# Two images instead of four summed by TensorE, and an earlier row of finishes on VectorE

## Chip, cores and metric

One Trainium2 chip, one of its cores. The metric is the device time of one launch in microseconds (us), as the median of the runs shown.

## What is computed

The input `x` has 16 images of 128 channels and 32 x 32 pixels, in fp32.

```python
cA, cH, cV, cD = dwt2(x)                     # one level of the Haar wavelet
rimg0 = idwt2(proc(cA), proc(cH), proc(cV), proc(cD))   # 1x1 conv, batch norm, ReLU on each band
rimg1 = idwt2(r2, h1, v1, d1)                # three levels there and back: x again
y = conv3x3(concat([rimg0, rimg1])) + convW_b
x = batchnorm_relu(y, bnW_gamma, bnW_beta)   # the second batch norm, over all 16 images
x_denoised = median_blur(x, 3)               # median of each 3x3 neighbourhood, zero padding
out = x + einsum('bchw,oc->bohw', x_denoised, W) + b
```

## The kernel before

Channels lie on the 128 partitions, so an image is a tile of 128 x 1024. The engines run programs written out by hand, which meet at semaphores; nothing schedules them but the order of the code.

The first 364 us are the wavelet, the first batch norm and the 3x3 convolution on TensorE (PE). VectorE (DVE) takes the medians of the *unnormed* convolution output while PE convolves the images behind it, since a batch norm with its sign taken out keeps the order of the values. The 16 images are cut into 20 units (images 0, 1, 14 and 15 in halves); `median` runs once per unit, in 18 DVE instructions (L780 to L842).

This case is about the end, after the last convolution matmul. There the second batch norm's scale and shift become known (`second_batch_norm`, L884 to L908 on DVE), and then for each image `n`, in order:

- ScalarE (ACT) norms the median, `norm_median` (L622).
- GpSimd (POOL) zeroes the four corner pixels (L348), which releases PE; for an image in `OWN` it then makes the normed image itself in place, `map_x1` (L339).
- PE multiplies the median by `w2`, `mix` (L469), into one of the two halves of `conv_ps`, by turns. `mix(n)` therefore waits until the product of image `n-2` has been read.
- DVE adds the image, the product and the bias, `finish` (L914), and SyncE (SP) sends the image out.

For an image in `SUMMED` the way is another: ACT makes the normed image (L627), PE adds it to the product by a multiplication with a unit matrix (L472), and ACT carries the sum out (L630). Neither POOL's `map_x1` nor DVE's `finish` runs for it.

DVE comes to this end with three pieces of median work still to do: the second half of image 14 (rows of 128x288 and 128x576), the first half of image 15 (128x224 and 128x448) and its second half (288 and 576 again). Its instructions are counted as they are issued (all but L781, L823 and the closing L842 of a whole image); `second_batch_norm` is put after the counted step `BN3_AT`, and one `finish` after each counted step in `FINISH_AT`, for the images of `OWN` in turn. Below, "step 16" is a counted step. Steps 1 to 15 lie in the first of the three pieces, 16 to 31 in the second, 32 to 46 in the third. What is left of the finishes follows the last median. The median of image 15 is whole only then, so ACT, POOL, PE, DVE and SP take it through in a row after it.

Thirty matmuls of zeros (L479) keep PE busy between the last convolution matmul and the first `mix`.

Of the kernel before, what the change touches and what calls it, by code (L numbers as in the profile page):

```python
# [5 lines left out]
def wavelet_conv_median_kernel(nc, x, w1_t, w3_t, w2_t, vectors, out):  # L6
# [39 lines left out]
    BY_POOL = tuple(n for n in range(IMAGES) if n not in BY_DVE)  # L46


    SUMMED = (3, 6, 9, 12)
    OWN = [n for n in range(IMAGES) if n not in SUMMED]  # L50

    BN3_AT, FINISH_AT = 7, (16, 19, 22, 25, 28, 31, 34, 37, 40)


    HALVED = (0, 1, IMAGES - 2, IMAGES - 1)
# [11 lines left out]
    with ctx:  # L67
# [122 lines left out]
        def slot(n):  # L190
            first = n * (ROWS * W) + W
            return y[:, first:first + PIX]

        def zslot(n):
            return z[:, n, :]
# [31 lines left out]
        def _(sp):  # L227
# [17 lines left out]
            for n in range(IMAGES - 1):  # L245
                if n in SUMMED:
                    sp.wait_ge(out_by_act, SUMMED.index(n) + 1)
                else:
# [104 lines left out]
        def _(pe):  # L353
# [108 lines left out]
            def mix(n, k):  # L462
                if n > 0:
                    pe.wait_ge(med_ready, n)
                for b in range(2):
# [3 lines left out]
                    mm = nc.tensor.matmul(conv_ps[:, k, half], w2[:, :], zslot(n)[:, half], start=True, stop=n in OWN)  # L469
                    if n in SUMMED:  # L470
                        pe.wait_ge(x1_by_act, SUMMED.index(n) + 1)
                        mm = nc.tensor.matmul(conv_ps[:, k, half], unit[:, :], slot(n)[:, half], start=False, stop=True)  # L472
# [12 lines left out]
            for n in range(2, IMAGES):  # L485
                if n - 2 in SUMMED:
                    pe.wait_ge(out_by_act, SUMMED.index(n - 2) + 1)
# [475 lines left out]
```

## Time and profile before

| | |
|---|---|
| median of 3 runs | 418.46 us (416.7, 418.46, 418.57) |
| the profiled execution's own time | 418.77 us |
| its span in the profile | 416.3 us |
| busy over the span | PE 402.1, DVE 371.4, POOL 192.2, ACT 157.3 us |
| mean granted PE clock | 0.996 of 2.4 GHz |

The span reaches from the first to the last instruction of the core; the own time has 2.5 us more around it. Busy times overlap, so they say who is loaded, not who is waited for.

### The profile page before, as it was taken

The page shows a single profiled execution, that of the slowest core. Times are in us where ns is not written, and L with a number is a line of the kernel's source. Part 1 is how long each engine was busy: PE and PEld are TensorE (multiplying, and loading weights), DVE is VectorE, ACT ScalarE, POOL GpSimd, SP SyncE. Part 2 cuts the span into 40 slices and gives each one's busy share as a digit, 9 for nine tenths or more (in the row PEclk, how much of TensorE's full clock was granted, in tenths as well). Part 3 has the DMA queues.
Part 4 walks back from the last instruction along what each step waited for, and adds up shares of the span by engine and source line. Part 5 has one row for each costly group of instructions (what it writes and reads, how often), then busy time and mean ns, then how long its engine had stood idle before and what let it go on. Part 6 is the DMA issues. An engine that isn't in the chain of part 4 may idle for free.

```text
span 416.3 us, 3679 instructions
## 1 busy us (share of the span) xinstructions
PE 402.1 (97%) x1142; PEld 213.1 (51%) x1142; DVE 371.4 (89%) x528; ACT 157.3 (38%) x352; POOL 192.2 (46%) x196
## 2 busy tenths in 40 slices
PE   7889999999999999999999999999999999997994
PEld 2334578956444444444444444444446688843441
DVE  2899866999849999999999998989898999988995
ACT  1466663422253432323232323141413322373861
POOL 3999386531715543435554443434343440032341
PEclk9999999999999999999999999999999999999998
DMA  7980110010101011010101010100100000003654
GB/s 282 418 333 3 47 54 2 9 41 0 53 0 50 1 50 30 22 50 0 50 2 51 0 50 3 50 14 37 39 13 2 0 0 2 0 0 151 252 211 193
DMA packets 7794, 26.70 MB, mean 64 GB/s; under 512 B 992, under 2 KB 1248, under 8 KB 7776
## 3 DMA queue, kind: packets, MB, share of 16 engines
q1 hardware_dynamic: 7776, 26.48, 16.7%
q8 instruction: 9, 0.15, 0.2%
q14 instruction: 9, 0.07, 0.1%
HBM read 18.09 MB, written 8.39 MB: 64 GB/s over the span
## 4 chain that ended last, share of the span: by engine, by line
PE 86%; DVE 7%; ACT 2%; issue 2%; DMA 1%; POOL 1%; SPq 0%; POOLq 0%; DVEq 0%; ACTq 0%
PE conv_ps L380 75%; PE conv_ps L469 4%; PE one_ps L362 4%; PE one_ps L445 2%; PE conv_ps L472 1%; DVE z L660 1%; DVE z L661 1%; DVE stats L666 1%; DMA z<-x 1%; DVE y L914 1%; POOL y L339 1%; ACT z L622 1%; ACT sorted_cols L503 0%; ACT y L627 0%; ACT y L630 0%
## 5 line engine op out<-in xcount | busy, mean ns | idle before, releaser
L380 PE MATMUL conv_ps<-ru,wt 128*128 128x512 f32 (+1 forms) x360 | 131.2, 500 | 0.0
L380 PEld LDWEIGHTS conv_ps<-ru,wt 128*128 128x128 f32 x360 | 68.2, 190 | 53.3 <-issue 50.2
L380 PE MATMUL conv_ps<-xu,wt 128*128 128x496 f32 (+3 forms) x240 | 87.4, 500 | 0.0
L573 ACT ACTIVATE y<-conv_ps,sgn 128x512 f32<-128x512 f32 (+1 forms) x40 | 25.5, 637 | 161.5 <-PE conv_ps L380 161.5
L380 PEld LDWEIGHTS conv_ps<-xu,wt 128*128 128x128 f32 x240 | 45.5, 190 | 35.4 <-issue 33.2
L313 POOL TENSOR_TENSOR ru<-eo 128x512 f32<-128x512 f32 x16 | 17.0, 1061 | 86.5 <-DVE one_ps L781 86.3
L221 POOL TENSOR_TENSOR ru<-z 128x512 f32<-128x512 f32 x14 | 18.0, 1289 | 59.5 <-DVE one_ps L823 59.5
L380 PE MATMUL conv_ps<-ru,v 128*128 128x496 f32 (+3 forms) x120 | 43.7, 500 | 0.0
L380 PE MATMUL conv_ps<-y,v 128*128 128x496 f32 (+3 forms) x108 | 38.6, 491 | 0.0
L380 PE MATMUL conv_ps<-y,wt 128*128 128x496 f32 (+3 forms) x108 | 38.6, 491 | 0.0
L469 PE MATMUL conv_ps<-z,w 128*128 128x512 f32 x64 | 31.3, 624 | 5.7 <-DVE y L914 3.4
L362 PE MATMUL one_ps<-y,w 128*128 128x512 f32 x64 | 32.0, 638 | 3.9 <-DVE z L661 2.5
L539 ACT ACTIVATE z<-z,bn 128x256 f32<-128x256 f32 x64 | 33.0, 590 | 1.2 <-DVE bn L726 1.2
L380 PEld LDWEIGHTS conv_ps<-ru,v 128*128 128x128 f32 x120 | 22.8, 190 | 18.0 <-issue 16.8
L380 PEld LDWEIGHTS conv_ps<-y,wt 128*128 128x128 f32 x108 | 20.5, 190 | 16.1 <-issue 15.3
L380 PEld LDWEIGHTS conv_ps<-y,v 128*128 128x128 f32 x108 | 20.4, 190 | 16.3 <-issue 14.8
L566 ACT ACTIVATE p_kept<-conv_ps 128x512 f32<-128x512 f32 (+1 forms) x20 | 10.2, 512 | 48.0 <-PE conv_ps L380 48.0
L780 DVE TENSOR_TENSOR one_ps<-y 128x512 f32<-128x512 f32 (+2 forms) x20 | 11.8, 589 | 17.3 <-ACT y L573 17.3
L579 ACT ACTIVATE conv_ps<-conv_ps,neg_shift,sgn 128x512 f32<-128x512 f32 (+1 forms) x40 | 26.3, 658 | 0.0
L307 POOL TENSOR_TENSOR eo<-ru 128x512 f32<-128x512 f32 x16 | 20.7, 1291 | 9.3 <-DVE ru L738 8.1
L469 PEld LDWEIGHTS conv_ps<-z,w 128*128 128x128 f32 x64 | 12.2, 198 | 22.5 <-DVE y L914 10.6
L362 PEld LDWEIGHTS one_ps<-y,w 128*128 128x128 f32 x64 | 11.8, 201 | 21.7 <-issue 17.4
(127 smaller groups left out, 663.9 us busy)
## 6 DMA issues: line engine op xcount, KB each, us to landing
z<-x SPq DMA_DIRECT2D x16, 512.0 KB, 10.5
raw<-x SPq DMA_DIRECT2D x16, 512.0 KB, 3.3
out<-y SPq DMA_DIRECT2D x15, 512.0 KB, 2.6
wt<-w_t SPq DMA_DIRECT2D x2, 576.0 KB, 10.0
out<-y SPq DMA_DIRECT2D x2, 256.0 KB, 2.0
w<-w_t SPq DMA_DIRECT2D x2, 64.0 KB, 7.9
vec<-vectors SPq DMA_DIRECT2D x1, 3.0 KB, 9.1
```

The lines of the kernel that those rows point to most:

```text
L221: v.tensor_tensor(even_rows(ru12[n % 2][:, :]), a_v, h_d, ALU.add)
L307: G.tensor_tensor(even, u1, u2, ALU.add)
L313: G.tensor_tensor(at(ru03[k][:, :], 0, [[BW, H], [1, BW]]), left, odd, ALU.subtract)
L362: mm = nc.tensor.matmul(one_ps[:, n % 2, b * BANK:(b + 1) * BANK], w1[:, :], slot(n)[:, b * BANK:(b + 1) * BANK], start=True, stop=True)
L380: return nc.tensor.matmul(bank(u, b)[:, (r0 - row) * BW:(r1 - row) * BW], taps(half, kx, ky), plane[:, (r0 + dy) * BW:(r1 + dy) * BW], sta ...
L445: mm = nc.tensor.matmul(one_ps[:, i, b * BANK + r0 * BW:b * BANK + r1 * BW], taps(X_HALF, (None, 1)[b], ky), planes(slot(n))[b][:, (r0 + d ...
L469: mm = nc.tensor.matmul(conv_ps[:, k, half], w2[:, :], zslot(n)[:, half], start=True, stop=n in OWN)
L539: ins = S.activation(band, band, ACT.Relu, bias=bn1[:, 5, b:b + 1], scale=bn1[:, 4, b:b + 1])
L566: S.activation(p_kept[u % 2][:, 0:cols], conv_ps[:, u % 2, 0:cols], ACT.Identity).then_inc(p_copied, 1)
L573: S.activation(at(slot(n), row * W + b, [[2, cols]]), src, ACT.Identity, scale=sgn[:, :], accum_out=y_sum[:, part:part + 1]).then_inc(y_ke ...
L579: S.activation(src, src, ACT.Square, bias=neg_shift[:, :], scale=sgn[:, :], accum_out=y_sq[:, part:part + 1]).then_inc(squares_summed, 1)
L780: step(V.tensor_tensor(sorted_rows(0), even, odd, ALU.min))
```

## The change

`SUMMED` loses images 3, 6 and 12 and gains 4, with 9 kept: 14 images instead of 12 go through `map_x1` and `finish`. `second_batch_norm` moves from behind step 7 to behind step 9, and the finishes, 11 instead of 9 of them, stand at steps 13 to 43.

```diff
-    SUMMED = (3, 6, 9, 12)
+    SUMMED = (4, 9)
     OWN = [n for n in range(IMAGES) if n not in SUMMED]
-    BN3_AT, FINISH_AT = 7, (16, 19, 22, 25, 28, 31, 34, 37, 40)
+    BN3_AT, FINISH_AT = 9, (13, 16, 19, 22, 25, 28, 31, 34, 37, 40, 43)
```

DVE, at the second batch norm (L886 to L908) in the first of the three pieces; L914 is a finish, `-` is before and `+` is the change:

```order
 L813 TENSOR_TENSOR one_ps<-sorted_cols 128x288
 L815 TENSOR_TENSOR one_ps<-sorted_cols 128x288
+L817 TENSOR_TENSOR one_ps<-one_ps,sorted_cols 128x576
+L819 TENSOR_TENSOR z<-one_ps,sorted_cols 128x576
 L886 TENSOR_REDUCE y_total<-y_sum 128x1
...
 L908 SCALAR_TENSOR_TENSOR shift<-mid,neg_scale,vec 128x1
-L817 TENSOR_TENSOR one_ps<-one_ps,sorted_cols 128x576
-L819 TENSOR_TENSOR z<-one_ps,sorted_cols 128x576
 L821 TENSOR_TENSOR one_ps<-sorted_cols 128x288
```

Two median steps now stand ahead of the norm. A little further on, and again near the end of the third piece, a finish is put in; all other finishes stand at the median steps where one stood before. Here is the first of the two places, at step 13:

```order
 L830 TENSOR_TENSOR sorted_cols<-one_ps,sorted_cols 128x18x32
 L832 TENSOR_TENSOR one_ps<-one_ps,z 128x576
+L914 SCALAR_TENSOR_TENSOR y<-y,vec,conv_ps 128x1024
 L834 TENSOR_TENSOR sorted_cols<-one_ps,sorted_cols 128x18x32
 L838 TENSOR_TENSOR one_ps<-one_ps,sorted_cols 128x576
```

So the finish at step 16 is that of image 1 and no longer of image 0, and so on; from step 31 (image 7) on, both kernels finish the same image at the same step, and step 43 is added for image 12.

ACT, from the norm of image 1 on (`L622` is a median's norm, `L627` the image's norm, `L630` the carrying out of a summed image); these rows are the changed kernel's up to the second image that is carried out, with those of before under `-`:

```order
 L618 ACTIVATE z<-z,shift,scale 128x512 x2
+L622 ACTIVATE z<-z,shift,scale 128x1024 x4
+L627 ACTIVATE y<-y,shift,scale 128x1024
+L622 ACTIVATE z<-z,shift,scale 128x1024 x2
+L630 ACTIVATE y<-conv_ps,vec 128x1024
 L622 ACTIVATE z<-z,shift,scale 128x1024 x3
 L627 ACTIVATE y<-y,shift,scale 128x1024
 L622 ACTIVATE z<-z,shift,scale 128x1024 x2
 L630 ACTIVATE y<-conv_ps,vec 128x1024
-L622 ACTIVATE z<-z,shift,scale 128x1024
-L627 ACTIVATE y<-y,shift,scale 128x1024
```

Behind each carrying out there are now at least three median norms in a row, where before one norm was followed by L627.

## Rows read from the trace of the kernel before

**Rows 1.** Windows: us, then busy us (and count) of each engine, PE clock, DMA.
```profile
60.00:364.00 304.00, 304.00 (x893) 168.89 (x892) 283.45 (x356) 98.38 (x251) 131.16 (x118) 1.00 0.06 21
364.00:408.00 44.00, 39.72 (x107) 16.80 (x105) 39.29 (x72) 27.83 (x30) 15.03 (x27) 1.00 0.38 155
```

**Rows 2.** Timeline of DVE around the second batch norm: start, us, instruction, [idle before].
```profile
363.72 0.46 DVE L815 TENSOR_TENSOR one_ps<-sorted_cols 128x288 f32<-128x288 f32 x1
365.28 0.20 DVE L886 TENSOR_REDUCE y_total<-y_sum 128x1 f32<-128x40 f32 x1 [1.11 <-ACT conv_ps L579]
...
367.67 0.76 DVE L817 TENSOR_TENSOR one_ps<-one_ps,sorted_cols 128x576 f32<-128x576 f32 x1
...
369.00 0.46 DVE L821 TENSOR_TENSOR one_ps<-sorted_cols 128x288 f32<-128x288 f32 x1
```

**Rows 3.** Timeline of PE from the first mix on.
```profile
370.41 3.60 PE L469 MATMUL conv_ps<-z,w 128*128 128x512 f32 x8
...
379.37 1.12 PE L469 MATMUL conv_ps<-z,w 128*128 128x512 f32 x2 [1.77 <-DVE y L914]
...
382.91 4.46 PE L469 MATMUL conv_ps<-z,w 128*128 128x512 f32 x10
...
409.39 3.60 PE L469 MATMUL conv_ps<-z,w 128*128 128x512 f32 x4 [2.28 <-POOL z L348]
```

**Rows 4.** Timeline of DVE through the finishes.
```profile
371.73 0.75 DVE L834 TENSOR_TENSOR sorted_cols<-one_ps,sorted_cols 128x576 f32<-128x576 f32 x1
...
373.99 0.39 DVE L780 TENSOR_TENSOR one_ps<-y 128x224 f32<-128x224 f32 x1
374.29 1.27 DVE L914 SCALAR_TENSOR_TENSOR y<-y,vec,conv_ps 128x1024 f32<-128x1024 f32 x1
375.48 1.06 DVE L781 TENSOR_TENSOR one_ps<-y 128x224 f32<-128x224 f32 x1
...
378.05 1.27 DVE L914 SCALAR_TENSOR_TENSOR y<-y,vec,conv_ps 128x1024 f32<-128x1024 f32 x1
...
384.89 1.28 DVE L914 SCALAR_TENSOR_TENSOR y<-y,vec,conv_ps 128x1024 f32<-128x1024 f32 x1 [1.88 <-PE conv_ps L469]
386.09 0.40 DVE L823 TENSOR_TENSOR one_ps<-sorted_cols 128x224 f32<-128x224 f32 x1
...
391.76 1.28 DVE L914 SCALAR_TENSOR_TENSOR y<-y,vec,conv_ps 128x1024 f32<-128x1024 f32 x1 [0.64 <-PE conv_ps L469]
...
398.63 1.28 DVE L914 SCALAR_TENSOR_TENSOR y<-y,vec,conv_ps 128x1024 f32<-128x1024 f32 x1 [0.62 <-PE conv_ps L469]
399.82 0.46 DVE L815 TENSOR_TENSOR one_ps<-sorted_cols 128x288 f32<-128x288 f32 x1
...
407.04 0.76 DVE L842 TENSOR_TENSOR z<-one_ps,sorted_cols 128x576 f32<-128x576 f32 x1
```

**Rows 5.** Timeline of ACT: norms of images 1 to 3, and a carrying out.
```profile
369.21 3.49 ACT L622 ACTIVATE z<-z,shift,scale 128x1024 f32<-128x1024 f32 x3
...
383.11 1.12 ACT L630 ACTIVATE y<-conv_ps,vec 128x1024 f32<-128x1024 f32 x1 [7.01 <-PE conv_ps L472]
384.12 1.23 ACT L622 ACTIVATE z<-z,shift,scale 128x1024 f32<-128x1024 f32 x1
```

**Rows 6.** Timeline of POOL in the same stretch.
```profile
375.10 1.20 POOL L339 TENSOR_SCALAR y<-y,scale,shift_bias 128x1024 f32<-128x1024 f32 x1
...
385.41 0.10 POOL L348 MEMSET z<- 128x4 f32 x1 [7.81 <-ACT z L622]
```

**Rows 7.** Timeline of DVE, 66 to 70 us.
```profile
66.79 1.46 DVE L781 TENSOR_TENSOR one_ps<-y 128x224 f32<-128x224 f32 x1
```

**Rows 8.** Timeline of POOL, 66 to 70 us.
```profile
66.49 1.50 POOL L307 TENSOR_TENSOR eo<-ru 128x512 f32<-128x512 f32 x1
```

**Rows 9.** Windows of one us, columns as in Rows 1.
```profile
378.00:379.00 1.00, 0.00 (x0) 0.00 (x0) 1.00 (x2) 0.00 (x0) 0.00 (x0) 1.00 0.00 0
...
410.00:411.00 1.00, 1.00 (x2) 0.34 (x1) 0.18 (x1) 0.00 (x0) 0.41 (x1) 0.50 1.04 418
```

## Prediction

> **What bounds it now.** I read the windows by stage first. Up to 364 us PE is busy all the time [rows 1], and the change touches nothing there. From 364 to 408 us PE is busy for 39.7 of 44 us and DVE for 39.3 [rows 1]: neither is the bound by its busy time, so I went through the timelines of both and asked at each finish who waits. Their waits alternate. DVE waits 1.11 us for the last squares ahead of the second batch norm [rows 2] and 1.88, 0.64 and 0.62 us for products at three finishes [rows 4]; PE waits 1.77 us for a finish [rows 3]. What decides the end is when DVE is through with the last median (L842, 407.80 us) [rows 4]: ACT norms it, POOL sets its corners, PE multiplies it at 409.39 [rows 3], and the two half finishes and their transfers take the rest up to 416.3 us. That tail of 8.5 us is the same in both kernels, and the two whole finishes in it run beside ACT and POOL. So I count by how much L842 moves. DVE is a queue in fixed order, so each of its waits and each added instruction goes into that time, unless a later wait for PE swallows it.
>
> **The change, step by step on DVE.** Times without a mark are those of before; "now" is the changed kernel.
>
> 1. *Batch norm behind L819.* L817 and L819 take 369.00 - 367.67 = 1.33 us [rows 2]. L815 is at 363.72 and lasts 0.46, and the next row starts some 0.09 before such a row's end (L780 at 373.99 lasts 0.39, L914 follows at 374.29 [rows 4]); so L817 starts at 364.09 now and L819 is through at 365.42. The squares are there by 365.28, so the norm is 0.14 late. It takes 367.67 - 365.28 = 2.39 us and L821 starts at 367.81 in place of 369.00: **-1.19**. The 1.11 us wait is filled with work; what is 0.14 late is ACT's and POOL's start on the norms.
>
> 2. *A finish at step 13.* It stands ahead of L834, which was at 371.73, so DVE is there at 370.54 now. The first product cannot be ready: PE starts it at 370.41, right behind the 30 matmuls of zeros, which the change doesn't move. From a `mix`'s first matmul to its finish there are 384.89 - 382.91 = 1.98 us [rows 3, 4]. The finish of image 0 starts at 372.39 now: a new wait of 1.85, and the finish itself, 375.48 - 374.29 = 1.19. Behind it on DVE are all the medians. **+3.04.** Balance at step 16: +1.85, the finish there now at 376.14.
>
> 3. *L781 behind the finish of step 16.* Before, it took 1.06 us where L780 of the same size took 0.39 [rows 4]. POOL's `map_x1` of 375.10 was running [rows 6]; taking L781's own 0.39 off its end leaves 376.15, so it was held for the first 1.05 us of that. Early in the kernel the same line takes 1.46 us [rows 7] beside a POOL instruction that ends at 67.99 [rows 8]; 66.79 + 1.46 - 0.39 = 67.86. I read both as one thing: a DVE step with both inputs in SBUF stands still while POOL is in an instruction of its own. Now L781 comes at 377.33. ACT's norms are (3.49 - 1.23) / 2 = 1.13 apart [rows 5]; image 5's is the sixth in its row, at 369.35 + 5 x 1.13 = 375.00; the corners follow 1.29 later (384.12 to 385.41 [rows 5, 6]) and `map_x1` some 0.1 behind, at 376.4. It lets go at 377.4, so L781 stands for 0.08: **-0.59.** Balance +1.26.
>
> 4. *The finish at step 25, behind the summed image 4.* The finish at step 19 (378.05) ends at 379.32 + 1.26 = 380.58 now, and frees the half that image 4 needs. A summed image takes PE 382.91 - 379.37 = 3.54 us [rows 3], as image 3 did: PE is through with it at 384.17, and image 5's finish can start at 386.15, 1.26 later than the 384.89 of before. The 1.88 us wait stays whole: **0.** PE needs 3.4 us less in all, but of images 3 and 4 one is still summed, at the same place in DVE's queue.
>
> 5. *L823 behind it.* ACT carries image 4 out from 384.37 (0.20 behind PE, as at 383.11), norms image 7 at 385.38, POOL sets corners at 386.67 and maps image 7 from about 386.75 [rows 5, 6]. L823 comes at 386.15 + 1.20 = 387.35, inside it, and has both inputs in SBUF. By step 3 it stands until 387.81: **+0.46.** Before, ACT's next image was a summed one, POOL had no map to do there, and L823 took its 0.40 [rows 4]. Balance +1.72.
>
> 6. *The finish at step 31.* Before it waited 0.64 behind the summed image 6 [rows 4]. Now image 6 is an ordinary one; image 7's product is ready near 389.6 (384.17, three products of four rows, 0.43 apart by [rows 3] (4.46 less 3.60 for two more rows), and the 0.26 that 1.98 has over 1.72), and DVE comes at 391.76 - 0.64 + 1.72 = 392.84. **-0.64.** Balance +1.08.
>
> 7. *The finish at step 37, behind the summed image 9.* Image 9 starts when the finish of image 7 ends, 394.12 and 0.05 now; plus 3.54 and 1.98 is 399.69 against 398.63. The wait of 0.62 stays nearly whole (DVE is there at 399.09): **-0.02.** L815 behind it, 0.46 long before [rows 4], meets POOL's map of image 12 just as L823 met that of image 7: **+0.47.** Balance +1.53.
>
> 8. *A finish at step 43.* Its product is ready near 403, DVE comes past 406, so only the 1.19 of the finish count: **+1.19.**
>
> The sum is **+2.7 us**. The other edits cost nothing: two more maps on POOL lie in its idle time (15.0 of 44 us busy [rows 1]) but for the stops counted; ACT has less to do; SP's transfers keep their order. Without the port's stops (3, 5 and 7) the sum is +1.7.
>
> The Trainium skill bears on those stops. Its page "SBUF — State Buffer", section "Who interferes with whom", says that a VectorE instruction with two SBUF inputs contends with a GpSimd instruction that reads SBUF, and whichever came first has the port until it is done. By that rule the sum is +2.7; if the 1.06 us row were a hitch of its own, it would be +1.7. The rows of L781 agree with the rule.
>
> The span of 416.3 us becomes 419.0, and the profiled execution's 418.77 becomes 421.5. That execution lay 0.3 above the median, so I predict **421.2 us**, +0.65%.
>
> **Rivals.** By a measurement of this kernel some 0.5%, 2.1 us, can be told from no change.
>
> *A. The stops at POOL don't come, or fall elsewhere.* POOL's maps are placed by three chained starts; if a map starts behind L823 and L815 instead, POOL waits and not DVE. Against it: in steps 5 and 7 both sides hang on the same end of a summed product, and DVE's step falls 0.6 us into a map of 1.2. +1.7, 420.2 us: no difference to be told. Chance 0.17.
>
> *B. The last product runs at the other clock.* The product at 409.39 takes 3.60 us for four rows, where two images together (x8) took as much at 370.41 [rows 3], and the granted clock is 0.50, the 1.2 GHz level, after 2.28 us without a matmul [rows 3, 9]. At the full clock it would be about 1.7 us shorter. The fastest run before, 416.7, is 1.8 below the others: I take it (an estimate) for one with that product at full clock. If the changed kernel's middle run is such a one: 419.5 us, no difference to be told. Chance 0.15.
>
> *C. TensorE's clock falls earlier too.* PE now has a gap before most products: 1.4 us and more before images 3, 8, 13 and 14, where before it ran through from 379 to 407. For it: the share of busy time falls from nine tenths to about seven. Against it: at 378 us, inside a gap of 1.77, the clock was 1.00 [rows 3, 9], and none of the new gaps but the last is longer. A product at 1.2 GHz takes 1.7 more, and it counts where DVE waits (images 0, 5, 10): 422 to 423 us. Chance 0.10.
>
> *D. Not slower: PE's saved time arrives.* If PE were through with its products before DVE asks at steps 13, 25 and 37, the waits of 1.85, 1.9 and 0.6 would go, and the sum would be +2.7 - 4.35 = -1.6, 416.9 us. The point that decides is step 25: a summed product must start 1.9 us earlier than the finish of image 2 allows, and I see no row that gives it that. Chance 0.06.
>
> **The numbers.** The sum as worked out has 0.50 (420.5 to 421.9), A 0.17, B 0.15, C 0.10, D 0.06, others 0.02. Slower: the first and C, a little over 0.6. Same: A, B and most of D, 0.34. Faster needs more than D gives: 0.04. The range goes from B to C's lower end: 419.4 to 422.8.
>
> **What would show it.** L886 with no wait ahead at 365.4; the first finish at 372.4 with some 1.85 us of idle ahead of it for PE; L781 near 0.45; a wait near 1.9 at the finish of image 5, none at image 7, 0.6 at image 10; L823 and L815 behind them at 0.85 us; L842 ending near 410.5. It is wrong if the finish of image 5 finds its product ready, if the two small steps take their 0.40 and 0.46, or if the clock is below 1.00 anywhere between 374 and 408 us.

## The result: 0.7% slower

| | before | changed |
|---|---|---|
| median of 7 runs | 418.46 us | 420.68 us (420.04 to 421.38) |
| ratio to before | 1 | 1.0071, 95% interval 1.0049 to 1.0092 |
| profiled execution, own time | 418.77 us | 420.47 us |
| its span | 416.3 us | 418.1 us |
| end of the last L842 | 407.80 us | 410.22 us |
| PE, DVE busy from 364 to 408 us | 39.7, 39.3 us | 35.9, 39.3 us |

The prediction was 421.2 us, +0.65%, with a range of 419.4 to 422.8. The ratio is the one on record; the two medians alone give 1.0053, because the times before lie in two groups, two at 416.7 and five at 418.3 to 418.9 us, and the median falls into the upper one. The same kernel measured once more, on another chip, gave 420.26 us there, 1.0073 (1.0050 to 1.0097) times the kernel before.

Such groups go with the granted clock of PE. In the 59 runs of the kernel before that stand beside the experiments, its mean over the span was 1.000 in 33 (medians of 416.1 to 416.5 us, by chip) and 0.994 to 0.996 in 26 (418.4 to 418.6 us); in all 17 runs of the changed kernel it was 0.993 to 0.996. So medians and ratios hold when the clock fell as well as what the engines wait for.

Executions differ by up to 1.2 us in when their convolution ends. So in all that follows a place in the tail is counted from the start of the thirty matmuls of zeros (363.93 us before, 363.79 in the changed kernel), which directly follow the last convolution matmul. Six of the traces of the experiments lack the record of the first of the thirty: they have 30 weight loads and 29 matmuls, as this view of the kernel with the norm back at step 7 shows.

```profile
L479 PEld LDWEIGHTS conv_ps<-zeros x30: 98/98/98, 363.6 to 369.9; 128*128 128x128 bf16 x30
L479 PE MATMUL conv_ps<-zeros x29: 379/379/379, 364.0 to 370.1; 128*128 128x512 bf16 x29
```

For these six the start is put one matmul's spacing, 0.22 us, ahead of the first that is recorded. By that measure the last L842 ended at 43.87 us before and at 46.43 now: **2.56 us later**, where the sum said 2.7.

### The profile page after: what moved, and what is told of

It reads as the page before. It is cut to its first block, busy times and chain, and to the rows that moved or that the text cites. A ratio compares the mean times of both kernels' runs of the same rounds, so it can differ in the third digit from the quotient of the medians.

```text
span 418.1 us, 3665 instructions
## 1 busy us (share of the span) xinstructions
PE 398.9 (95%) x1134; PEld 211.0 (50%) x1134; DVE 374.7 (90%) x530; ACT 152.7 (37%) x348; POOL 193.5 (46%) x198
## 4 chain that ended last, share of the span: by engine, by line
PE 85%; POOL 5%; DVE 4%; issue 3%; DMA 2%; ACT 1%; SPq 0%; POOLq 0%; DVEq 0%
PE conv_ps L380 75%; PE one_ps L362 3%; PE conv_ps L469 3%; PE one_ps L445 2%; DVE y L914 2%; POOL y L214 2%; POOL y L215 2%; DMA z<-x 2%; PE conv_ps L479 2%; POOL y L339 1%; PE conv_ps L472 1%; DVE one_ps L838 0%; SPq L231 0%; DVE sorted_cols L834 0%; ACT z L622 0%
## 5 line engine op out<-in xcount | busy, mean ns | idle before, releaser
L380 PE MATMUL conv_ps<-y,wt 128*128 128x496 f32 (+3 forms) x108 | 38.6, 491 | 0.0
L380 PE MATMUL conv_ps<-y,v 128*128 128x496 f32 (+3 forms) x108 | 38.6, 491 | 0.0
L780 DVE TENSOR_TENSOR one_ps<-y 128x512 f32<-128x512 f32 (+2 forms) x20 | 12.8, 639 | 16.5 <-ACT y L573 16.5
L914 DVE SCALAR_TENSOR_TENSOR y<-y,vec,conv_ps 128x1024 f32<-128x1024 f32 (+1 forms) x15 | 17.9, 1201 | 5.9 <-PE conv_ps L469 5.9
```

Source lines behind the costliest of these rows:

```text
L380: return nc.tensor.matmul(bank(u, b)[:, (r0 - row) * BW:(r1 - row) * BW], taps(half, kx, ky), plane[:, (r0 + dy) * BW:(r1 + dy) * BW], sta ...
L780: step(V.tensor_tensor(sorted_rows(0), even, odd, ALU.min))
L914: V.scalar_tensor_tensor(v, v, cb2, conv_ps[:, n % 2, first:first + count], ALU.max, ALU.add).then_inc(out_ready, 1)
```

## The profile after

The timeline of DVE, around the second batch norm and the first finish, which answers to [rows 2] and the first line of [rows 4]:

```profile
363.94 0.75 DVE L817 TENSOR_TENSOR one_ps<-one_ps,sorted_cols 128x576 f32<-128x576 f32 x1
364.61 0.74 DVE L819 TENSOR_TENSOR z<-one_ps,sorted_cols 128x576 f32<-128x576 f32 x1
365.27 0.18 DVE L886 TENSOR_REDUCE y_total<-y_sum 128x1 f32<-128x40 f32 x1
...
367.64 0.46 DVE L821 TENSOR_TENSOR one_ps<-sorted_cols 128x288 f32<-128x288 f32 x1
...
372.25 1.28 DVE L914 SCALAR_TENSOR_TENSOR y<-y,vec,conv_ps 128x1024 f32<-128x1024 f32 x1 [1.79 <-PE conv_ps L469]
373.45 0.75 DVE L834 TENSOR_TENSOR sorted_cols<-one_ps,sorted_cols 128x576 f32<-128x576 f32 x1
```

L886 no longer waits, L821 comes 1.2 us earlier in its execution, and then the finish of image 0 waits at the head of DVE's queue for 1.79 us. The saved time is in that wait. Further on, the same view:

```profile
376.01 1.27 DVE L914 SCALAR_TENSOR_TENSOR y<-y,vec,conv_ps 128x1024 f32<-128x1024 f32 x1
377.21 0.43 DVE L781 TENSOR_TENSOR one_ps<-y 128x224 f32<-128x224 f32 x1
...
379.15 1.26 DVE L914 SCALAR_TENSOR_TENSOR y<-y,vec,conv_ps 128x1024 f32<-128x1024 f32 x1
...
385.99 1.28 DVE L914 SCALAR_TENSOR_TENSOR y<-y,vec,conv_ps 128x1024 f32<-128x1024 f32 x1 [1.88 <-PE conv_ps L469]
387.19 0.83 DVE L823 TENSOR_TENSOR one_ps<-sorted_cols 128x224 f32<-128x224 f32 x1
...
392.58 1.27 DVE L914 SCALAR_TENSOR_TENSOR y<-y,vec,conv_ps 128x1024 f32<-128x1024 f32 x1
...
399.43 1.28 DVE L914 SCALAR_TENSOR_TENSOR y<-y,vec,conv_ps 128x1024 f32<-128x1024 f32 x1 [0.62 <-PE conv_ps L469]
400.63 0.90 DVE L815 TENSOR_TENSOR one_ps<-sorted_cols 128x288 f32<-128x288 f32 x1
...
406.04 1.26 DVE L914 SCALAR_TENSOR_TENSOR y<-y,vec,conv_ps 128x1024 f32<-128x1024 f32 x1
...
409.46 0.76 DVE L842 TENSOR_TENSOR z<-one_ps,sorted_cols 128x576 f32<-128x576 f32 x1
```

Against [rows 4]: of the three waits of before the 1.88 and 0.62 are still there and the 0.64 is gone (image 7, at 392.58). L781 is back at 0.43, and L823 and L815, 0.40 and 0.46 before, take 0.83 and 0.90. POOL shows why; its timeline:

```profile
386.58 1.20 POOL L339 TENSOR_SCALAR y<-y,scale,shift_bias 128x1024 f32<-128x1024 f32 x1
...
400.02 1.19 POOL L339 TENSOR_SCALAR y<-y,scale,shift_bias 128x1024 f32<-128x1024 f32 x1
```

L823 starts 0.61 us into the first of these maps and L815 0.61 into the second. On PE there is now idle time before products between 379 and 407 us, where it ran through before (the second of these lines is one of them):

```profile
377.34 1.98 PE L469 MATMUL conv_ps<-z,w 128*128 128x512 f32 x4 [1.76 <-DVE y L914]
...
390.86 1.98 PE L469 MATMUL conv_ps<-z,w 128*128 128x512 f32 x4 [1.54 <-DVE y L914]
...
411.80 3.04 PE L469 MATMUL conv_ps<-z,w 128*128 128x512 f32 x4 [2.47 <-POOL z L348]
```

The first two products took 1.98 us, at the full clock; the last one took 3.04, against 3.60 before. The windows (columns as in [rows 1]) show a granted clock of 1.00 up to 408 us and its fall inside the last product:

```profile
364.00:408.00 44.00, 35.88 (x96) 14.66 (x95) 39.32 (x71) 23.16 (x25) 16.62 (x29) 1.00 0.35 143
...
411.00:412.00 1.00, 0.20 (x1) 0.23 (x2) 1.00 (x2) 0.50 (x1) 0.45 (x2) 1.00 0.00 0
...
413.00:414.00 1.00, 1.00 (x3) 0.27 (x1) 0.75 (x1) 0.00 (x0) 0.00 (x0) 0.50 1.00 401
```

Behind L842 the span goes on for 7.9 us here and for 8.5 before: 0.55 us less, which the change did not bring. 2.56 - 0.55, less the 0.14 us by which this execution's convolution ended earlier, are the 1.87 us by which the span grew (416.26 to 418.13 us).

## The experiments

Theory: DVE's fixed queue sets the end. What DVE waits, what it is stopped by POOL and what is added to it moves the last L842, unless a wait further on was going to last until a fixed time anyway. Main rival: PE's products set the end, and a wait taken away at one finish comes back at the next. "L842" is the end of the last one, counted as above.

| kernel | L842 | to before | to changed | median | times before (95% interval) |
|---|---|---|---|---|---|
| before | 43.87 | | -2.56 | 418.46 | |
| changed | 46.43 | +2.56 | | 420.68 | 1.0071 (1.0049 to 1.0092) |
| changed, measured again | 46.46 | +2.59 | +0.03 | 420.26 | 1.0073 (1.0050 to 1.0097) |
| norm back at step 7 | 46.40 | +2.5 | -0.03 | 420.25 | 1.0076 (1.0050 to 1.0102) |
| norm alone | 42.27 | -1.6 | | 415.54 | 0.9955 (0.9937 to 0.9974) |
| first finish at 15 | 44.82 | | -1.61 | 417.73 | 1.0010 (0.9991 to 1.0030) |
| two maps blank | 45.59 | | -0.84 | 418.68 (one run) | |
| two finishes later | 45.06 | | -1.37 | 417.82 | 1.0021 (0.9997 to 1.0045) |
| zeros at the end | 46.44 | | 0.0 | 419.39 | 1.0059 (1.0038 to 1.0080) |
| images alone | 42.91 | -1.0 | | 420.90 | 1.0101 (1.0064 to 1.0137) |
| two summed, retimed | 41.78 | -2.1 | -4.65 | 414.37 | 0.9928 (0.9900 to 0.9956) |
| four summed, retimed | 39.42 | -4.4 | -7.01 | 412.25 | 0.9882 (0.9851 to 0.9914) |

Each ratio is to the kernel before on the same chip, where its median was 416.7 to 417.3 us (418.46 us for the row "changed"). L842 is the column to compare by, since the medians also hold the clock of the last product.

**The norm back behind step 7.**

```diff
-    BN3_AT, FINISH_AT = 9, (13, 16, 19, 22, 25, 28, 31, 34, 37, 40, 43)
+    BN3_AT, FINISH_AT = 7, (13, 16, 19, 22, 25, 28, 31, 34, 37, 40, 43)
```

> The changed kernel with the second batch norm back behind step 7. Theory (a queue with waits that swallow): the 1.2 us that the norm's place saves on DVE ends in the wait of the first finish at step 13, which sets the same start (about 372.2 us) either way. So that wait falls from 1.79 us to about 0.6, L886 waits 1.1 us again, L842 ends within 0.3 us of the changed kernel's 410.2, and the time stays near 420.7 us (420.2 to 421.2). Rival (the terms of the sum add up each by itself): 1.2 us slower, near 421.9 us.

The timeline of DVE:

```profile
365.18 0.20 DVE L886 TENSOR_REDUCE y_total<-y_sum 128x1 f32<-128x40 f32 x1 [1.10 <-ACT conv_ps L579]
...
372.29 1.28 DVE L914 SCALAR_TENSOR_TENSOR y<-y,vec,conv_ps 128x1024 f32<-128x1024 f32 x1 [0.58 <-PE conv_ps L469]
```

The wait at L886 is 1.1 us again, that of the first finish is 1.2 us shorter, and L842 is where it was, within 0.03 us. In the changed kernel the norm's place is worth nothing.

**The norm alone**, in the kernel before.

```diff
-    BN3_AT, FINISH_AT = 7, (16, 19, 22, 25, 28, 31, 34, 37, 40)
+    BN3_AT, FINISH_AT = 9, (16, 19, 22, 25, 28, 31, 34, 37, 40)
```

> The kernel before with only the norm moved behind step 9; four images summed, finishes at their old places. Theory: nothing waits at step 16 (the product is ready at 372.4, DVE comes at 373.1), so the whole 1.2 us reach the end: L842 ends near 406.4 (before 407.80), the wait of 1.88 us at step 25 stays, the time is near 417.1 us, and up to 0.6 us more is gained if L781 no longer meets POOL's map. Rival: the finishes' waits for PE swallow it (the chain there is PE's), and the time stays at 418.5 us.

The timeline of DVE:

```profile
372.35 0.67 DVE L780 TENSOR_TENSOR one_ps<-y 128x224 f32<-128x224 f32 x1
...
374.12 0.39 DVE L781 TENSOR_TENSOR one_ps<-y 128x224 f32<-128x224 f32 x1
...
382.87 1.28 DVE L914 SCALAR_TENSOR_TENSOR y<-y,vec,conv_ps 128x1024 f32<-128x1024 f32 x1 [1.88 <-PE conv_ps L469]
```

Here no finish stands at step 13, and the time arrives: L842 ends 1.6 us earlier. That is the 1.2 of the norm's place and 0.4 from a stop: L781 takes 0.39 us again, 0.67 less than in [rows 4], and L780 ahead of it gives 0.28 of that back. The waits at steps 25, 31 and 37 are 1.88, 0.63 and 0.62, as before: they moved with DVE, as the theory says, and swallowed nothing. The rival falls. The median of 415.54 us is 1.6 below the expected one; behind L842 the span went on for 7.3 us in place of 8.5.

**The first finish at step 15.**

```diff
-    BN3_AT, FINISH_AT = 9, (13, 16, 19, 22, 25, 28, 31, 34, 37, 40, 43)
+    BN3_AT, FINISH_AT = 9, (15, 16, 19, 22, 25, 28, 31, 34, 37, 40, 43)
```

> The changed kernel with the first finish at step 15 in place of 13; two steps of 0.78 and 0.80 us then stand ahead of it, in the time that it waited. Theory: its wait falls from 1.79 to about 0.2 us, and L842 ends 1.6 us earlier, near 408.6; the time is near 419.1 us, a little less or more by the clock of the last product. Rival: the product, not DVE, is what the later finishes wait for, so that the wait comes back at step 25, and the time stays at 420.7 us.

The timeline of DVE:

```profile
372.17 1.28 DVE L914 SCALAR_TENSOR_TENSOR y<-y,vec,conv_ps 128x1024 f32<-128x1024 f32 x1 [0.31 <-PE conv_ps L469]
...
384.29 1.28 DVE L914 SCALAR_TENSOR_TENSOR y<-y,vec,conv_ps 128x1024 f32<-128x1024 f32 x1 [1.88 <-PE conv_ps L469]
```

The first finish has waited 0.31 us, the wait at step 25 is still 1.88, so nothing came back there and the rival falls; L842 ends 1.61 us earlier, as expected. One number in the table of steps took back nearly two thirds of what L842 had lost. The median of 417.73 us is below the expected 419.1; the mean clock was 1.000 in 7 of these 10 runs.

**Two maps blank.**

```diff
-                G.tensor_scalar(slot(n), slot(n), scale3[:, :], shift3_bias2[:, :], ALU.mult, ALU.add).then_inc(x1_by_pool, 1)
+                if n in (7, 12):
+                    G.memset(slot(n), 0.0).then_inc(x1_by_pool, 1)
+                else:
+                    G.tensor_scalar(slot(n), slot(n), scale3[:, :], shift3_bias2[:, :], ALU.mult, ALU.add).then_inc(x1_by_pool, 1)
```

> The changed kernel in which POOL's map of images 7 and 12 is left out and a memset of the same tile, which reads nothing, stands in its place, so that these two images come out without their own part. Theory (two SBUF inputs on DVE against a read by POOL): L823 behind the finish of image 5 takes 0.40 us in place of 0.83, L815 behind that of image 10 0.46 in place of 0.90, and L842 ends 0.9 us earlier, near 409.3, if the 0.43 is not taken back by the wait at the finish of image 10. Rival (any POOL instruction on that tile, or the start of an output transfer, holds DVE): both stay above 0.8 us.

The lines of this kernel below the edit stand three further down, so L826 is the step that was L823 and L818 the one that was L815. Timelines of DVE and of POOL:

```profile
387.33 0.39 DVE L826 TENSOR_TENSOR one_ps<-sorted_cols 128x224 f32<-128x224 f32 x1
...
400.33 0.48 DVE L818 TENSOR_TENSOR one_ps<-sorted_cols 128x288 f32<-128x288 f32 x1
```

```profile
386.69 0.95 POOL L340 MEMSET y<- 128x1024 f32 x1
...
399.68 0.95 POOL L340 MEMSET y<- 128x1024 f32 x1
```

Both steps still start inside a POOL instruction that writes the tile that the map wrote (386.69 to 387.64, 399.68 to 400.63), and neither is held. The stops hang on POOL's *reading*; together they are worth 0.84 us at L842, against 0.9 expected. The Trainium skill's page "SBUF — State Buffer", section "Who interferes with whom", states just this: two inputs in SBUF contend with a GpSimd instruction that reads SBUF, and not with one that only writes it. The runs agree: 0.83 and 0.90 us against a map, 0.39 and 0.48 against a memset.

**Two finishes later.**

```diff
-    BN3_AT, FINISH_AT = 9, (13, 16, 19, 22, 25, 28, 31, 34, 37, 40, 43)
+    BN3_AT, FINISH_AT = 9, (13, 16, 19, 22, 26, 28, 31, 34, 38, 40, 43)
```

> The changed kernel with the finishes of images 5 and 10 one counted step later (26 and 38), behind L828 and L815. L823, L828 and L815 then run while DVE would wait for the products, and before POOL's maps of images 7 and 12. Theory: L823 and L815 take 0.40 and 0.46 us, the waits fall from 1.88 to about 1.0 and from 0.62 to about 0, and L842 ends about 1.6 us earlier, near 408.6; time near 419.1 us. Rival (what follows on PE is late by as much, and the gain is given back at the next finishes): 420.7 us.

The two small steps now run ahead of the maps, and the waits fall to 1.05 and below 0.1. But DVE's arrival is shifted against POOL, and a third step runs into a map; timelines of DVE and POOL:

```profile
391.45 1.33 DVE L780 TENSOR_TENSOR one_ps<-y 128x288 f32<-128x288 f32 x1
```

```profile
391.28 1.19 POOL L339 TENSOR_SCALAR y<-y,scale,shift_bias 128x1024 f32<-128x1024 f32 x1
```

L780 of this size takes 0.46 us free, so it lost 0.87. The two stops (0.87) and 1.4 us of waits went, and 0.87 came back: 1.37 us were won where 1.6 were expected. The median of 417.82 us is below the expected 419.1; the mean clock was 1.000 in 8 of these 10 runs.

**The images alone.** The kernel before with `SUMMED = (4, 9)` and nothing else.

> The kernel before with only the choice of the summed images changed to (4, 9); the norm behind step 7 and nine finishes at the old places, so that three whole finishes are left behind the last median. Theory: the waits at steps 25 and 37 stay (about 1.2 and 1.0 us), that of 0.64 at step 31 goes, L842 ends near 407, but the products of images 13 to 15 come late since the finish of image 11 stands behind L842; the time is 418.5 to 420.5 us, so most of what the change loses is lost by the choice of the images and not by the finishes' places. Rival (the finish at step 13 is the loss): 416.5 to 417.5 us.

L842 is 1.0 us earlier than before, and yet the kernel is no faster than the changed one: 1.0101 times before, with an interval that overlaps the other's. The median of 420.90 us is above the expected range. Only nine finishes stand in the medians, for 14 images: the finish of image 11 comes behind L842, the products of images 13 to 15 behind it, so four whole finishes are left there and not three. The two waits came as expected in size, 1.14 and 0.99 us, but at steps 28 and 40, where the finishes of images 5 and 10 stand in this list. The timeline of PE:

```profile
375.03 2.85 PE L469 MATMUL conv_ps<-z,w 128*128 128x512 f32 x4 [2.01 <-DVE y L914]
...
407.11 6.91 PE L469 MATMUL conv_ps<-z,w 128*128 128x512 f32 x12 [4.63 <-DVE y L914]
```

Two things are to be seen. PE stands still for 4.63 us waiting for that finish, and what follows L842 takes 12.2 us instead of some 8. And the clock fell in the middle of the tail, as rival C had it: the product at 375.03, behind 2.01 us of idle, took 2.85 us, and in the window from 376 to 378 us the granted clock is 0.50. So the expectation's reading, that the choice of the images is the loss, can't be had from this run: it is the choice together with a list that is too short for it.

**Two summed, retimed; four summed, retimed.** Eleven finishes for images (4, 9), and nine for (3, 6, 9, 12), put where the product is ready when DVE arrives, worked out from the durations above.

```diff
-    BN3_AT, FINISH_AT = 9, (13, 16, 19, 22, 25, 28, 31, 34, 37, 40, 43)
+    BN3_AT, FINISH_AT = 9, (15, 16, 18, 20, 26, 29, 32, 34, 40, 41, 43)
```

> Two images summed (4, 9) and the norm behind step 9 as in the changed kernel, but the eleven finishes at steps 15, 16, 18, 20, 26, 29, 32, 34, 40, 41, 43, placed like those of the four-image version, so that their products are there. Theory: the waits fall from 4.3 to about 0.8 us and L842 ends 2.5 to 2.9 us earlier than in the changed kernel, near 407.6; what is left above the four-image version's 403.1 are two finishes of 1.2 us and stops at POOL. Time 417.0 to 418.5 us: no difference to before that can be told. Rival (two fewer products on PE are worth it once the places are right): below 415 us.

```diff
-    BN3_AT, FINISH_AT = 7, (16, 19, 22, 25, 28, 31, 34, 37, 40)
+    BN3_AT, FINISH_AT = 9, (15, 16, 17, 24, 28, 32, 35, 40, 43)
```

> Four images summed as before (3, 6, 9, 12), the norm behind step 9, and the nine finishes at steps 15, 16, 17, 24, 28, 32, 35, 40, 43, each chosen by the rows of before so that its product is there when DVE comes. Theory (DVE's queue sets the end and its waits are what is to be won): no finish before the last median waits more than 0.4 us, L842 ends 4 to 4.5 us earlier than before's 407.80, and PE, which then hardly stands still, keeps its clock to the end; the time is 412.5 to 414.5 us. Rival (PE is the bound as soon as the waits go, or the stops at POOL move to other steps): 416 to 418 us.

With two summed images L842 came 4.65 us earlier than in the changed kernel, where 2.5 to 2.9 were expected. The expectation had some 2.1 us of stops at POOL in it (407.6 less 403.1 and two finishes of 1.2), which did not come. The waits that are left are 0.32 and 0.52 us. DVE and POOL still meet; timelines of DVE and of POOL:

```profile
389.58 0.47 DVE L781 TENSOR_TENSOR one_ps<-y 128x288 f32<-128x288 f32 x1
```

```profile
389.48 1.46 POOL L339 TENSOR_SCALAR y<-y,scale,shift_bias 128x1024 f32<-128x1024 f32 x1
```

Four maps here take 1.46 to 1.50 us in place of 1.20. Behind the start of each, by 0.02 to 0.10 us, starts a DVE step with two inputs in SBUF, and none of the four steps is held: POOL is the one that loses time, and no finish behind these maps waits for it. The kernel is 0.7% faster than before, so the choice of the images alone is not what made the changed kernel slower. Its 414.37 us are the time that the rival gave, but not for the rival's reason: with four summed images, two more for PE to sum, the retimed kernel ends its L842 earlier still. With four, L842 ends at 39.42, 4.4 us ahead of before, as expected, and the kernel is 1.2% faster than before (the expected range began at 412.5 us): the lowest median of all. Its windows:

```profile
364.00:403.00 39.00, 38.61 (x104) 16.35 (x102) 38.24 (x71) 27.48 (x29) 14.21 (x27) 1.00 0.41 166
```

DVE is busy for 38.2 of 39 us now and PE for 38.6: with the waits gone, both are. One stop is left (L781, 0.91 us at 375.45). The 2.36 us between the two retimed kernels are the two finishes of 1.19 us that two more images in `OWN` put on DVE.

**Zeros at the end.** On PE, ahead of the last product:

```diff
+                if n == IMAGES - 1:
+                    pe.wait_ge(med_made, IMAGES)
+                    for _ in range(6):
+                        nc.tensor.matmul(one_ps[:, 1, 0:BANK], zeros[:, 0:CH], zeros[:, :], start=True, stop=True)
```

> The changed kernel with six matmuls of zeros on PE (into the bank that the medians have done with) between the last median and the product of image 15. Theory of the clock: PE's 2.47 us of idle ahead of the last product let the granted clock fall to 0.50 inside it; with the zeros the product runs at 1.00, its four rows take about 1.98 us in place of 3.04, and the time is 0.5 to 1.1 us shorter, 419.6 to 420.2 us. Rival: the clock falls all the same, and the time stays near 420.7 us.

The timeline of PE:

```profile
411.64 1.96 PE L469 MATMUL conv_ps<-z,w 128*128 128x512 f32 x4
```

The last product took 1.96 us and the span went on for 6.85 us behind L842; the clock was 1.00 through the product, and the median of 419.39 us is just below the expected range. That looks like the theory, but the changed kernel's second profile has this:

```profile
411.92 1.96 PE L469 MATMUL conv_ps<-z,w 128*128 128x512 f32 x4 [2.47 <-POOL z L348]
```

The same 2.47 us of idle without any zeros, and the clock stayed. So the run shows what the full clock is worth at this place (behind L842, 6.85 us against 7.9 and 8.5), and not that the zeros keep it. The two ratios, 1.0059 and 1.0073 times before, lie inside each other's intervals. The mean clocks of all runs leave it open as well: with the zeros it is 0.998 or more in 9 of 10 runs, in the changed kernel in none of 17; but with the first finish at step 15, without zeros and with the same 2.47 us of idle, it is 1.000 in 7 of 10. And a mean doesn't tell where the clock fell: in the changed kernel's second profile the 0.996 comes from the first 20 us, with a clock of 0.91.

> The changed kernel itself, once more, beside the last one and the kernel before on one chip. Expected 420.0 to 421.4 us, and L842 at the same place; the clock of the last product may fall at another moment, which would show in the stretch behind L842 alone (7.9 us in the first profile, 6.85 at full clock, 8.5 if it falls ahead of the product).

L842 ended at 46.46 us there, against 46.43 in the first profile, and the waits (1.77, 1.88, 0.60) and the stops (0.84, 0.90) were the same.

## Why the prediction was right, by its steps

1. *Norm behind L819, -1.19:* L821 at 3.85 us behind the zeros' start, 5.07 before: -1.22. Right as a row. As an account of what the edit is worth it is wrong: undone alone it moved L842 by 0.03 us. It and the 1.85 of step 2 are one thing; without the norm's move that wait would have been 0.58. The sum came out because both were in it.
2. *A finish at step 13, +3.04:* a wait of 1.79 (1.85 said) and 1.20. At step 16 the balance was +1.86, said +1.85. Moving it to step 15 gave 1.61 back.
3. *L781, -0.59:* 0.43 us, down from 1.06; balance at step 19 +1.24, said +1.26. The reading behind it, that a DVE step with two inputs in SBUF stands still during any instruction of POOL's, is too wide: the memsets of the blank maps held nothing, and in the retimed kernel with two images POOL was the one held.
4. *The wait at step 25 stays* (image 4 before, image 5 now): 1.88 both times; balance +1.24. This is the step in which PE's 3.4 us less of work bring nothing, and rival D with it falls.
5. *L823, +0.46:* 0.83 us against 0.40, and the blank maps show the cause.
6. *Image 7 doesn't wait, -0.64:* it doesn't; balance +0.96, said +1.08.
7. *Image 10 waits on, L815 +0.47:* 0.62 again, and 0.90 against 0.46; balance at step 37 +0.94, said +1.06.
8. *A finish at step 43, +1.19:* no wait; L842 at +2.56, said +2.7.

In the profiled execution the span was 418.13 us where 419.0 had been said: 0.15 us are in the sum, 0.14 in the convolution's earlier end and 0.55 in the tail, which the prediction took as the same in both kernels. Its last product ran in part at the full clock, 3.04 us here against 3.60 in the execution that I counted from. The 0.5 us between the medians said and measured can't be split in the same way, as the other runs have no trace; that the miss is so small is in part luck, since the tail was 8.5, 7.9 and 6.8 us in the three profiles of the two kernels. Rival B therefore came true by half in the profiled run, and wholly in the second profile (1.96 us); neither the median nor the mean clock says in how many of the other runs. Rival A did not come: both stops fell where they were said. Rival C did not come in the changed kernel, whose clock was 1.00 from 364 to 408 us, but its mechanism was there in the run with the images alone.

Two figures of the forecast don't follow from its own terms: A, B and most of D make about 0.37 for "same" and not 0.34, and the upper end of the range, 422.8, is not the lower end of C, which is 422. Neither bears on the sum.

## What to carry to other kernels

Where one engine with a fixed queue alternates between its own work and finishing other engines' products, work out for each finish when its product can be there at the earliest and put it behind that; a finish one or two steps too early costs its wait for all that is queued behind it, and a saving just ahead of such a wait is worth nothing. Taking work off a busy engine (PE, 3.4 us by the prediction's count) brought nothing here, where that engine waits for the one that gets the work: between the two retimed kernels it cost 2.36 us. And place VectorE steps with two inputs in SBUF apart from GpSimd instructions that read SBUF: here a step of 0.4 to 0.5 us that fell into a map lost 0.3 to 0.9 us, which shows as a longer step and not as a wait.

## What I had not expected of the hardware

The length of PE's idle stretch does not by itself tell whether the granted clock falls. It fell to 0.50 behind 2.01 us of idle (images alone, 375.03) and 2.28 us ([rows 3]), and stayed at 1.00 behind 1.76 us (changed kernel, 377.34) and through a whole product behind 2.47 us (its second profile). What decides it stays open; no run here varied it by itself.
